# The middle 16-bit part of the row maxima taken from the PSUM bank in a one-core transformer block on Trainium2

## The chip, the core and the metric

The kernel runs on one core of one Trainium2 chip. A core has five instruction streams that run side by side and meet only at semaphores: TensorE (PE in the rows; its weight loads are shown as PEld), VectorE (DVE), ScalarE (ACT), GpSimd (POOL) and SyncE (SP, which here only issues DMAs). The metric is the device time of one execution in microseconds (us), as the median of the runs. A second figure, the span, is the time from the first to the last instruction of the one execution that was profiled.

## What is computed

The reference embeds a batch of 8 images of 1024 tokens with 29 features each to 128 channels, adds a position table, and runs one transformer block: attention with 8 heads of 16 channels over chunks with a causal mask, then a mixture-of-experts feed-forward layer.

```python
scores = jnp.einsum('bhqd,bhkd->bhqk', Q, K)
mask = (1.0 - causal) * -100000.0
attn = jax.nn.softmax((scores + mask) / math.sqrt(d), axis=-1)
out = jnp.einsum('bhqk,bhkd->bhqd', attn, V)
```

A softmax over 1024 keys needs the maximum of each row of scores. What the change touches is how that maximum is handed on.

## The kernel before

**Tiling.** An image `i` (8 of them) is worked through in two halves of 512 tokens. In attention, a unit `u` is a group of 4 heads of one half: 4 units for an image, 32 in all. The scores are made twice. The first time (`score`, L546) TensorE writes a 128-row tile into one of two banks `bank_s`, and VectorE takes the row maximum out of it (L784 with the mask for tiles on the diagonal, L780 without). The second time (`prob`, L576) the transposed scores, with the maxima already subtracted, go to one of two banks `bank_p`, and ScalarE takes the exponential (L1051); GpSimd zeroes what the mask hides (L1213), and `weigh` (L594) multiplies by the values.

**How the maxima travel.** The subtraction is part of the second matmul: queries and keys are stacked as 16-bit parts in `q_stack` and `k_stack`, and three extra rows of `q_stack` hold the maximum of each query as three bfloat16 parts that add up to the float32 value. The step is called `turn`: TensorE transposes the maxima of a unit into `bank_m` (L559), and VectorE splits them in four instructions (L798 to L804): the high part `mrow_h`, the remainder `mrow_r` in float32, its high part `mrow_m`, and what is left of it, `mrow_l`. Then SyncE issues three DMAs (L449), after which the first `prob` of the unit can run. `bank_m` is one bank, used in turn by embedding, projections, transposes, gates and shared layer; the semaphore `m_taken` says when VectorE or ScalarE has finished reading it, and the next step of TensorE that writes it waits for that.

**The rest of an image.** `emb`, `turn1`, `q`, `k`, `v` make queries, keys and values; `to`, `ant`, `oproj`, `z2t`, `gates`, `counts`, `shared` and the routing (`route`, parts 0 to 4, 19 small VectorE instructions, L872 to L923) stand behind attention; `in` (L480 to L482, then a tanh on ScalarE, L1089, and two VectorE products, `gate` L936 and `hid` L945) and `expert` (L682 to L684, L1107, L955) are the feed-forward layer, `combine` its weighted sum (L1113, L1243 to L1249).

**What sets the order.** Each engine's order is a string in the table `ORDER`, one letter for a step: s a score (or the merging of two maxima), p a prob, w a weigh or a take of its result, e load and embedding, a the projections, t the turn of maxima, b the steps behind attention, f feed-forward, h shared, c combine, d DMAs of stacked queries and keys, i steps done once at the start. The n-th letter of a kind stands for the n-th step of that stream, so a letter that moves among its neighbours moves a step past those of other streams. A wait in a step holds up all that stands behind it on its engine. The steps done once, on SyncE the loading of ten tensors of weights (`load_rest`, L423), on VectorE the rounding of the query and key weights (`front_weights`, L967 and L970), on ScalarE the filling of three rows of keys (`first_keys`, L1138), are placed by the letter i. At the very end TensorE runs filler matmuls (L492).

## Time and profile before

| | |
|---|---|
| median of 3 runs | 950.03 us (949.52 to 952.06) |
| the profiled execution | 951.46 us, span 949.7 us |
| mean granted TensorE clock | 0.984 |
| PE busy | 907.3 us (96%) |
| DVE busy | 786.0 us (83%) |
| ACT busy | 596.3 us (63%) |
| POOL busy | 374.8 us (39%) |
| scores on VectorE, L784 and L780 | 244.3 and 166.0 us |
| the four instructions of the split, L798 to L804 | 8.7, 8.9, 9.2 and 10.2 us |

Of the profiled execution, 1.8 us lie outside the span (951.46 against 949.7). TensorE's busy time counts a matmul as the time it takes alone, so that neighbours overlap in the rows; a wait then shows on the weight loads (PEld) before it shows on the matmuls. VectorE's order is a queue of its own, and a row with `[x <-y]` says that the engine sat idle x us until y was done.

### The profile page before, as it was taken

What the parts mean: (1) busy time and instruction counts of PE and PEld (TensorE: products, weight loads), DVE (VectorE), ACT (ScalarE), POOL (GpSimd) and SP (SyncE); (2) the same over time, 40 slices, a digit from 0 to 9 for tenths busy, and PEclk for the clock granted to TensorE, in tenths of its full rate; (3) what the DMA queues carried; (4) which work ended last, traced back from release to release, by engine and by line L of the source; (5) the groups of instructions that cost most, each with busy time, mean ns of one, the idle gap of its engine ahead of it and who ended that gap; (6) DMA issues with size and microseconds to landing.
All of it is one profiled execution on the core that took longest, in us unless ns stands there. A gap on an engine that the chain in (4) does not pass through costs nothing. (4 is left out here: it accounts for less than half of the span.)

```text
span 949.7 us, 17664 instructions
## 1 busy us (share of the span) xinstructions
PE 907.3 (96%) x5646; PEld 540.7 (57%) x5646; DVE 786.0 (83%) x2529; ACT 596.3 (63%) x1365; POOL 374.8 (39%) x526
## 2 busy tenths in 40 slices
PE   7788999899999999999999999999999999999996
PEld 7633356356575656457555756466564765555575
DVE  5799988798789888889889889898889998894543
ACT  1335675475857675775766675675767576776644
POOL 3713323323445335343354325344444234332424
PEclk9799999899999999999999999999999999999999
DMA  5231011200111001110102001110110101000000
GB/s 178 59 54 50 20 35 34 65 16 4 34 46 57 10 18 49 38 65 18 35 15 72 26 24 40 45 47 30 38 46 17 47 26 46 26 13 2 12 1 23
DMA packets 45980, 35.19 MB, mean 37 GB/s; under 512 B 10816, under 2 KB 44608, under 8 KB 45760
## 3 DMA queue, kind: packets, MB, share of 16 engines
q1 hardware_dynamic: 43680, 31.97, 10.5%
q10 hardware_dynamic: 2208, 2.10, 1.0%
q8 instruction: 45, 0.74, 0.4%
q14 instruction: 47, 0.39, 0.1%
HBM read 4.28 MB, written 4.19 MB: 9 GB/s over the span
## 5 line engine op out<-in xcount | busy, mean ns | idle before, releaser
L1051 ACT ACTIVATE pt<-bank_p 128x512 f32<-128x512 f32 (+3 forms) x768 | 349.9, 492 | 200.6 <-PE bank_p L576 178.5
L784 DVE CUSTOM_DVE_ANT_0 bank_s<-bank_s,causal 128x384 f32<-128x384 f32 (+3 forms) x512 | 244.3, 505 | 40.0 <-PE bank_s L546 37.2
L546 PE MATMUL bank_s<-k_stack,q_stack 96*128 96x512 bf16 (+3 forms) x768 | 236.0, 333 | 17.4 <-DVE mx L784 8.9
L576 PE MATMUL bank_p<-q_stack,k_stack 99*128 99x512 bf16 (+3 forms) x768 | 229.0, 332 | 6.9 <-ACT pt L1051 5.1
L780 DVE TENSOR_REDUCE mx_far<-bank_s 128x1 f32<-128x512 f32 x256 | 166.0, 682 | 20.6 <-PE bank_s L546 19.2
L1213 POOL TENSOR_SCALAR_AFFINE_SELECT pt<-pt 128x512 f32<-128x512 f32 x128 | 81.1, 636 | 206.7 <-ACT pt L1051 206.5
L594 PE MATMUL bank_w<-pt,v 128*32 128x512 f32 (+3 forms) x1536 | 155.2, 502 | 0.2 <-POOL pt L1213 0.2
L546 PEld LDWEIGHTS bank_s<-k_stack,q_stack 96*128 96x128 bf16 x768 | 72.1, 99 | 131.9 <-DVE mx L784 55.6
L576 PEld LDWEIGHTS bank_p<-q_stack,k_stack 99*128 99x128 bf16 x768 | 72.7, 99 | 117.6 <-ACT pt L1051 69.8
L682 PE MATMUL bank_f<-wex_h,hid_h 128*128 128x512 f32 x256 | 116.4, 455 | 0.8 <-DVE gate L936 0.7
L684 PE MATMUL bank_f<-wex_h,hid_l 128*128 128x512 f32 x256 | 101.4, 396 | 0.0
L683 PE MATMUL bank_f<-wex_l,hid_h 128*128 128x512 f32 x256 | 101.2, 395 | 0.0
L1113 ACT ACTIVATE sel<-sel,wsel 128x128 f32<-128x128 f32 x256 | 81.5, 399 | 15.5 <-DVE sel L955 15.5
L784 DVE DVE_READ_ACCUMULATOR2_ANT mx<- 128x1 f32 x512 | 72.0, 141 | 0.0
L594 PEld LDWEIGHTS bank_w<-pt,v 128*32 128x32 f32 x1536 | 36.4, 109 | 62.5 <-issue 47.4
L1243 POOL TENSOR_TENSOR sel<-sel 128x256 f32<-128x256 f32 x64 | 46.8, 731 | 59.4 <-ACT sel L1113 59.4
L1107 ACT ACTIVATE sel<-bank_f,gm 128x512 f32<-128x512 f32 x64 | 44.0, 687 | 41.5 <-PE bank_f L684 21.8
L480 PE MATMUL bank_f<-z2t_h,win_h 128*128 128x512 f32 x128 | 66.6, 520 | 3.3 <-DVE gate L936 2.0
L1234 POOL TENSOR_TENSOR hid_l<-hid,hid_h 128x512 fp32r<-128x512 f32 x32 | 41.0, 1284 | 71.9 <-ACT hid_h L1097 71.9
L955 DVE SCALAR_TENSOR_TENSOR sel<-bank_f,gm,sel 128x512 f32<-128x512 f32 x64 | 47.7, 746 | 26.1 <-PE bank_f L684 16.5
L682 PEld LDWEIGHTS bank_f<-wex_h,hid_h 128*128 128x128 f32 x256 | 48.4, 189 | 13.2 <-issue 1.4
L684 PEld LDWEIGHTS bank_f<-wex_h,hid_l 128*128 128x128 f32 x256 | 48.1, 188 | 11.2
(139 smaller groups left out, 1428.9 us busy)
## 6 DMA issues: line engine op xcount, KB each, us to landing
q_stack<-qk_h SPq DMA_DIRECT2D x96, 64.0 KB, 2.6
k_stack<-qk_h SPq DMA_DIRECT2D x84, 64.0 KB, 2.6
q_stack<-qk_m SPq DMA_DIRECT2D x64, 64.0 KB, 2.6
out<-h SPq DMA_DIRECT2D x16, 256.0 KB, 2.4
k_stack<-qk_m SPq DMA_DIRECT2D x56, 64.0 KB, 2.6
q_stack<-qk_l SPq DMA_DIRECT2D x32, 64.0 KB, 2.6
k_stack<-qk_l SPq DMA_DIRECT2D x28, 64.0 KB, 2.4
x_sb<-x_t SPq DMA_DIRECT2D x16, 64.0 KB, 2.4
```

Of the source, the lines that this page charges most:

```text
L480: nc.tensor.matmul(dst, wh, xh, start=True, stop=False)
L546: nc.tensor.matmul(s_bank[s % 2][:, 0:cols], q_stack[0:STACK, half, hd, t % HT * P:(t % HT + 1) * P], k_stack[0:STACK, hd, key_place(i, ha ...
L576: nc.tensor.matmul(p_bank[p % 2][:, q0:HALF], k_stack[:, hd, key_place(i, kt // HT), kt % HT * P:(kt % HT + 1) * P], q_stack[:, half, hd, ...
L594: mm = nc.tensor.matmul(w_bank[VW * j:VW * (j + 1), q0:HALF], v[:, i % 2, kt, first:first + VW], pt[:, k % PT_SLOTS, j, q0:HALF], start=(k ...
L682: nc.tensor.matmul(f_bank[g][:], hid_h[:, c, tok], wex_h[:, c, w], start=(c == 0), stop=False)
L683: nc.tensor.matmul(f_bank[g][:], hid_h[:, c, tok], wex_l[:, c, w], start=False, stop=False)
L684: mm = nc.tensor.matmul(f_bank[g][:], hid_l[:, c, tok], wex_h[:, c, w], start=False, stop=(c == HID // P - 1))
L780: nc.vector.tensor_reduce(mx_far[:, u, col:col + 1], s_bank[s % 2][:], AX.X, ALU.max).then_inc(s_taken, 1)
L784: nc.vector.tensor_tensor_reduce(src, src, causal[:, HALF - cols:HALF], 1.0, -3.0e38, ALU.add, ALU.max, mx[:, u, col:col + 1]).then_inc(s_ ...
L1051: nc.scalar.activation(pt[:, k % PT_SLOTS, j, q0:HALF], p_bank[p % 2][:, q0:HALF], ACT.Exp, scale=0.25).then_inc(exp_done, 1)
L1113: nc.scalar.mul(sel[:, t % 2, part], sel[:, t % 2, part], wsel[:, t, e:e + 1]).then_inc(weighted, 1)
L1213: nc.gpsimd.affine_select(out=d, in_=d, compare_op=ALU.is_ge, fill=0.0, base=0, pattern=[[0, G4], [1, P]], channel_multiplier=-1).then_inc ...
```

## The change

In the step `turn` on VectorE, the instruction that rounds `mrow_r` to `mrow_m` is taken out. In its place the difference of bank and `mrow_h` is made twice, first written as bfloat16 into `mrow_m`, then as float32 into `mrow_r`. No wait stands between these two. The signal that `bank_m` may be written again comes with the second.

```diff
                 nc.vector.tensor_copy(mrow_h[:, u, :], src).then_inc(mh_made, 1)
                 dve.wait_ge(mh_made, n + 1)
+                nc.vector.tensor_tensor(mrow_m[:, u, :], src, mrow_h[:, u, :], ALU.subtract).then_inc(mm_made, 1)
                 nc.vector.tensor_tensor(mrow_r[:], src, mrow_h[:, u, :], ALU.subtract).then_inc(m_taken, 1)
                 dve.wait_ge(m_taken, after(i, "turn", u))
-                nc.vector.tensor_copy(mrow_m[:, u, :], mrow_r[:]).then_inc(mm_made, 1)
                 dve.wait_ge(mm_made, n + 1)
                 nc.vector.tensor_tensor(mrow_l[:, u, :], mrow_r[:], mrow_m[:, u, :], ALU.subtract).then_inc(ml_made, 1)
```

All five strings of `ORDER` are written anew, each with the same letters as before. Against the string of before, 1104 of TensorE's 2224 letters stand in another place, by 0.8 of a place on average over all letters, the farthest by 27; on VectorE it is 424 of 1301, on ScalarE 420 of 1142, on GpSimd 154 of 318, on SyncE 70 of 123. The beginnings of two of them:

```diff
     "dve": (
-        "ieaaeaaaaaaaeasesssssssassssassssasessstsssasasssassssssssssassssastssssassssasssssassasssssassasstsssss"
+        "eaeiaaaaaaaaeasesssssssassssasssssasesstsssassassasssssssssassssssatssssasssssassssassassasssssassastssss"
...
     "act": (
-        "aaaddfaaiaddppppppppppapppppapppapppwppppppppppppawpppppppbpppappppppppppppppapppppppbppppppppfppwpappfpf"
+        "iaaaddfaaaddpppppppppppapppapppapppppppwppppppppwapppppppbppppappppppppppppppppppppbppppppppfppwpappff"
```

The first place is VectorE's `turn` of unit 0, the first of 32 like it. Before:

```order
71 L798 CAST mrow_h<-bank_m 16x128
72 L800 TENSOR_TENSOR mrow_r<-bank_m,mrow_h 16x128
73 L802 CAST mrow_m<-mrow_r 16x128
74 L804 TENSOR_TENSOR mrow_l<-mrow_r,mrow_m 16x128
```

And with the change:

```order
71 L798 CAST mrow_h<-bank_m 16x128
72 L800 TENSOR_TENSOR mrow_m<-bank_m,mrow_h 16x128
73 L801 TENSOR_TENSOR mrow_r<-bank_m,mrow_h 16x128
74 L804 TENSOR_TENSOR mrow_l<-mrow_r,mrow_m 16x128
```

The cast from SBUF is gone, and two readings of the bank stand side by side.

The second place is VectorE about 39 us into the execution, where the remainders of the second half's queries are split (L759, L761) between scores of image 0. Before:

```order
58 L784 ISA bank_s,mx<-bank_s,causal 128x512
59 L784 ISA mx 128x1
60 L759 CAST qk_m<-qk_r 128x512
61 L761 TENSOR_TENSOR qk_l<-qk_r,qk_m 128x512
62 L784 ISA bank_s,mx<-bank_s,causal 128x128
```

And with the change:

```order
58 L784 ISA bank_s,mx<-bank_s,causal 128x512
59 L784 ISA mx 128x1
60 L784 ISA bank_s,mx<-bank_s,causal 128x128
61 L784 ISA mx 128x1
62 L759 CAST qk_m<-qk_r 128x512
63 L761 TENSOR_TENSOR qk_l<-qk_r,qk_m 128x512
```

One small score has gone ahead of the two.

The third place is VectorE near the end, where part 4 of the routing of the last image's first half (L914 to L923) meets the last products of its `in` steps (L936, L945). Before:

```order
2031 L945 SCALAR_TENSOR_TENSOR hid<-gate,bank_f 128x512
2032 L936 SCALAR_TENSOR_TENSOR gate<-gate,bank_f 128x512
2033 L914 TENSOR_TENSOR topp<-eprob,top 128x16
2034 L915 TENSOR_REDUCE esum<-eprob 128x4
2035 L917 TENSOR_REDUCE tsum<-topp 128x4
2036 L919 SCALAR_TENSOR_TENSOR tden<-esum,tsum 128x4
2037 L921 RECIPROCAL trec<-tden 128x4
2038 L923 TENSOR_TENSOR wsel<-topp,trec 128x16
2039 L945 SCALAR_TENSOR_TENSOR hid<-gate,bank_f 128x512
2040 L936 SCALAR_TENSOR_TENSOR gate<-gate,bank_f 128x512
2041 L945 SCALAR_TENSOR_TENSOR hid<-gate,bank_f 128x512
2042 L816 RECIPROCAL rec<-bank_m 128x16
```

And with the change:

```order
2029 L936 SCALAR_TENSOR_TENSOR gate<-gate,bank_f 128x512
2030 L945 SCALAR_TENSOR_TENSOR hid<-gate,bank_f 128x512
2031 L936 SCALAR_TENSOR_TENSOR gate<-gate,bank_f 128x512
2032 L945 SCALAR_TENSOR_TENSOR hid<-gate,bank_f 128x512
2033 L914 TENSOR_TENSOR topp<-eprob,top 128x16
2034 L915 TENSOR_REDUCE esum<-eprob 128x4
2035 L917 TENSOR_REDUCE tsum<-topp 128x4
2036 L919 SCALAR_TENSOR_TENSOR tden<-esum,tsum 128x4
2037 L921 RECIPROCAL trec<-tden 128x4
2038 L923 TENSOR_TENSOR wsel<-topp,trec 128x16
2039 L816 RECIPROCAL rec<-bank_m 128x16
```

The six instructions of the routing now stand behind both `hid` products instead of ahead of them.

Three of the steps done once have moved too. On VectorE `front_weights` stands behind the second embedding (L720) instead of ahead of the first. On ScalarE `first_keys` is the first step instead of the one between the second half's `q` and `k`. On SyncE the two loads of image 1's tokens (L417, each waiting for an embedding on TensorE) stand ahead of the ten loads of weights (L423) instead of behind them.

## Rows read from the trace of the kernel before

**Rows 1.** Windows: us, then busy time (and count) of each engine, clock, DMA, GB/s.
```profile
100.00:850.00 750.00, 735.66 (x4670) 429.49 (x4669) 661.15 (x2163) 502.73 (x1165) 299.19 (x423) 1.00 0.11 34
```

**Rows 2.** Waits, TensorE's weight loads: us in total, times, longest.
```profile
PEld bank_p L576 <- ACT pt L1051: 69.8, 160, 1.8
PEld bank_s L546 <- DVE mx L784: 55.6, 131, 3.3
PEld bank_s L546 <- DVE mx_far L780: 32.5, 79, 1.7
```

**Rows 3.** Groups of VectorE instructions: busy us, mean ns, idle before.
```profile
L804 DVE TENSOR_TENSOR mrow_l<-mrow_r,mrow_m 16x128 bf16<-16x128 f32 x32 | 10.2, 318 | 1.1
L802 DVE CAST mrow_m<-mrow_r 16x128 bf16<-16x128 f32 x32 | 9.2, 287 | 1.1
```

**Rows 4.** The tile mrow_r: durations min/median/max in ns; then who waited for it.
```profile
L800 DVE TENSOR_TENSOR mrow_r<-bank_m,mrow_h x32: 278/279/280, 45.1 to 860.5; 16x128 f32<-16x128 f32 x32
L802 DVE CAST mrow_m<-mrow_r x32: 214/215/752, 45.4 to 860.8; 16x128 bf16<-16x128 f32 x32
L804 DVE TENSOR_TENSOR mrow_l<-mrow_r,mrow_m x32: 278/280/612, 45.6 to 861.5; 16x128 bf16<-16x128 f32 x32
...
  PEld bank_m L480: 0.7, 2
```

**Rows 5.** Timeline of VectorE, one turn: start us, us, instruction.
```profile
613.16 0.28 DVE L800 TENSOR_TENSOR mrow_r<-bank_m,mrow_h 16x128 f32<-16x128 f32 x1
613.47 0.21 DVE L802 CAST mrow_m<-mrow_r 16x128 bf16<-16x128 f32 x1
613.72 0.28 DVE L804 TENSOR_TENSOR mrow_l<-mrow_r,mrow_m 16x128 bf16<-16x128 f32 x1
```

**Rows 6.** Timeline of GpSimd and VectorE, another turn.
```profile
334.82 0.73 POOL L1243 TENSOR_TENSOR sel<-sel 128x256 f32<-128x256 f32 x1
334.88 0.75 DVE L802 CAST mrow_m<-mrow_r 16x128 bf16<-16x128 f32 x1
335.67 0.57 DVE L804 TENSOR_TENSOR mrow_l<-mrow_r,mrow_m 16x128 bf16<-16x128 f32 x1
```

**Rows 7.** Timeline of VectorE and TensorE in the first 12 us.
```profile
5.67 0.36 DVE L967 CAST wqk_h<-z 128x128 fp32r<-128x128 f32 x2 [1.64 <-DMA bk_sb<-bk]
6.07 0.49 DVE L970 TENSOR_TENSOR wqk_l<-z,wqk_h 128x128 fp32r<-128x128 f32 x2
7.65 2.05 PE L508 MATMUL bank_m<-tokw_sb,x_sb 128*128 128x128 f32 x8 [0.95 <-DVE h L720]
10.40 1.12 DVE L738 TENSOR_SCALAR z<-h,mv,rs 128x128 f32<-128x128 f32 x4 [1.58 <-POOL rs L1190]
11.43 0.69 DVE L720 TENSOR_TENSOR h<-bank_m,pos_sb 128x512 f32<-128x512 f32 x1
```

**Rows 8.** Timeline of GpSimd, VectorE and TensorE, 36 to 44 us.
```profile
36.68 4.51 POOL L1255 TENSOR_TENSOR wex_l<-hid,wex_h 128x2048 fp32r<-128x2048 f32 x1
39.25 2.22 DVE L759 CAST qk_m<-qk_r 128x512 bf16<-128x512 f32 x1
43.06 0.29 DVE L784 CUSTOM_DVE_ANT_0 bank_s<-bank_s,causal 128x128 f32<-128x128 f32 x1
43.46 0.23 PE L546 MATMUL bank_s<-k_stack,q_stack 96*128 96x128 bf16 x1 [3.14 <-DVE mx L784]
```

**Rows 9.** Timeline of SyncE's queue and ScalarE at the start.
```profile
9.86 0.43 SPq L423 DMA_DIRECT2D bgate_sb<-b_gate  x1
28.54 1.04 ACT L1118 CAST win_h<-gate 128x1024 fp32r<-128x1024 f32 x1 [9.41 <-issue]
35.36 3.60 ACT L1138 CAST k_stack<-minus 3x4096 bf16<-3x4096 f32 x1
47.08 0.69 ACT L1032 ACTIVATE qk_h<-bank_m,bk_sb 128x512 bf16<-128x512 f32 x1 [8.12 <-PE bank_m L482]
```

**Rows 10.** Timeline of VectorE and TensorE, 893 to 900 us.
```profile
893.42 0.17 DVE L914 TENSOR_TENSOR topp<-eprob,top 128x16 f32<-128x16 f32 x1
895.63 0.68 DVE L945 SCALAR_TENSOR_TENSOR hid<-gate,bank_f 128x512 f32<-128x512 f32 x1
896.36 0.50 PE L480 MATMUL bank_f<-z2t_h,win_h 128*128 128x512 f32 x1 [1.05 <-DVE hid L945]
899.26 0.26 DVE L816 RECIPROCAL rec<-bank_m 128x16 f32<-128x16 f32 x1 [1.15 <-PE bank_m L612]
```

More of the change, by code:

```diff
@@ new lines @@
+        "hpsspwwsppsapsspssfssfsswstpswpspsasssspwsspepsswtspsspppspspsppspsbsppspspsppspbssswssbwwssbpspwppsapsp"
+        "wsppbswpssbsfpfptpfppsswpfppsswsfspassfpfsspfspfssfssbwsbspfbssppfsspbspfspsbpssfppswptpswphpwpsbspwsbps"
+        "pappfppfpfbwwppfepspfspspfpspwppwppsfpspsfpspasppfppfspsapsfphssfpspstfswwwspspfbsspfpsbfpspsbfspsbsppsf"
+        "psawpwssppwwppsaspspwpspstpsppeppswwppsbspswspsaspsffbspfpsafspfsppwpfsspfpfwspspbfsbpspfbssppfbfpssbspf"
+        "psphwsspfbpsspwwsppstfspsfpfppssbppssfpsspfpsfspapswwspspfswsppftspwpspwpsfasspfpspsfpsapssfspsapssfbpsp"
@@ new lines @@
+        "fsshspsfstfssfppsespfswwwwsppsapssppwpspspassppsswspspssppswssppwpspbspsppwppsspbpwpspstppswpspbsppswsbp"
+        "pspspepspspwppaspspwsppwbpswsspbppfspsfssppfapwwpbfsfbpfssbpfppsfbspfbpspfsppshspfpsbfssftssfpssbsppsfsp"
+        "sapsffpssaswwwwspspfppfssptpfsspasppfsfpspsaspsfpspsfspspwwwwsppsfsbppsfpsspfspsphpsspwssfsppstfpssffpss"
+        "fssppesswwwpspsbspspsppbspspwppbpspwspsbpspspwwpeppssppasppwspsppwsptspwpspbswssassffspapfpsfsbpspffassp"
+        "pfspswpspfwpssbfsbfbspspfbspfbpspsfpphspspfbpswwpssptwspsfspbspspfppsapspfpspswpspswwsppfpfssppftssppfsp"
@@ new lines @@
+        "sappsswwwsppsfsppsfspspfpspaspsfsspfsppsassppfbfsshsspfstfspsfssefspswwppswwspsaspsspswspspasppswpspbpps"
+        "swsppbppspsptpwspspbwpspsbpssppasppwsppwppsasppwpbsppswssbspsfppswpfbspfbspfppbfppsfbsfpsfpsbfppsshpspfb"
+        "ssfssbfpsptfesswwppsswwspsfbppssfppsfasppsffpssppapspsfspwwwssptfsppawspspfspsfpsspapspsfppswwspsfwspspf"
+        "tppsfspsfpspshppssfsppsfppssfssfpspsfspesswwwwssppspssppsbppwpspbpwsppsapswspsppbswsbppssppstppwppsapwpp"
+        "spsppwpspbspswpssaspsfsfppsbspffsspefspspfassppfwwwssppbffspsbfbpspsfbpssfsspphspfsspptfpssbpsspffsapsww"
@@ new lines @@
+        "fssssbsbsstbshsssbbfabsbfffsbssfsfessfssfsafssfasashsssfstssafbsssbssfssbsbfssabssssssastssesssssssasffb"
+        "sbfssffbsfsabfsfbssabssfsbssbsbssfbhsssfsssstassfssfssfssbssfsfssbassbstfsfbsbfssasfssssassasfssssfshsst"
+        "ssfseafssassssassssssssssssassssbsssbsstsssssbssbesssbasssssbbssfsbfbsbafafsbfsfbsfssafbsbfssbhssssfssst"
+        "ssfssbsbsbsabsbfssasfsfsstsfsfsasfssfsssssasfssfsssssfssshssssftssfssssfessasssbssbssasssbbssesssbsassst"
+        "ssssssasfsfasffssbfssasfbsbbsffsbsbsfbsassfbbssbhssasssstfsssssbbssbssfssfasfssfsstssfsfbsabssssfssfsssf"
@@ new lines @@
+        "sasssfasssfshssstssfsseafssasssssssasssassbsssbssstssssbsbsassbassssssbsbbsbfsfbbffsbsfsfssffsbbssbhsfss"
+        "sssbstfbssebabssssbfssasfssassfsfsasfstssfssassfsfssssssafsfstssfssshssfssssfsssssfesassssssabssbsssasss"
+        "ssbssbtssbsasssssssasfsfssbfssfebssfbsfsbfabsfsssbabfssssafssshssstssbfsbssfbasssssssassftfssbssbssbbsba"
+        "ssfsfsfssfssssssfsassfsfsssssfstsshsssssfssssfssbssbsssssbbstsssssbssssssbssbfsbfbfbfssfssfssfssfsssfsss"
+        "fsstbbbbbhfbfbbbffffffffbbfbbbhbfffbfbfbffffbffbffhff"
@@ new lines @@
+        "apppppppwppppapppppppppppppwppppbpppppppppppappwppbppppfbpppfpbfpfpfpfpbppppfpppcfpbfcpppfapfbappwppppfp"
+        "pfpappfpppppfpfpcppppbfppppccfppppfcpfpcpcpwppppppppppbppppppwpppppapppppppppbwafpapffppffppppbpfppbfppc"
+        "fbpppppcpppbfppppfppppppappppfbpppfppwpppffpapfcppppfpppcppapppfbcfpppfccfpppcppappppwapppppppppppppppbp"
+        "ppppwapppppppppbppwpfpppbbpfpfppffppbfppppppfbcfppfpbppcppbcppfapfppppppafpwpfpapppfpppfppppfcppppfppppc"
+        "pfpppppfcpcfcppwppppppppppppapppbwppppppppppapppppppbppapfppfpfpfwppfppbfbppfppcfppbpcppppfpppcfacpppbpp"
@@ L199 @@
+        "cfapacccpaacppcpppppppapbabfafappbcbpcpfafpcacpccppcaapppcpbppppbaaffabapcbpcppfcafcpapacpcapcppapppcpbp"
+        "pbffabpabcapcppfafcpcpaccpcapappppppbppcbaaffaaccppbpbpfapcfpapcppccppppcpbppcbffppppbcbcpppfpfccabccbff"
         "cccccc"
```

70 lines of the change are left out of this document (19 added, 51 removed).

## Prediction

> **What bounds the kernel now.** I read the windows first, since the busy shares of the page mix the start, the long middle and the end. Between 100 and 850 us TensorE is busy for 735.66 of 750 us, VectorE for 661.15, ScalarE for 502.73 and GpSimd for 299.19 [rows 1]. The reader should see two things: TensorE is nearly full, with 14.3 us of idle time in 750, and VectorE is second at 88%. So this is a kernel of two engines that hold each other up: TensorE sets the end, and it gets late where VectorE or ScalarE is late.
>
> The waits say how often. TensorE's weight loads waited 131 times for a masked maximum and 79 times for an unmasked one, 55.6 + 32.5 = 88.1 us in all, and 160 times for an exponential, 69.8 us [rows 2]. There are 768 scores, so in 210 / 768 = 27% of them VectorE was the last to be ready. I use that share below as the price of VectorE's time: of a microsecond that VectorE saves somewhere in the middle, about a quarter reaches TensorE. The chain that ended last covers only the final stretch here and carries no term.
>
> **The edit, on VectorE.** It stands in 32 places. In a turn without disturbance the remainder starts at 613.16, the cast 0.31 us behind it, the last difference another 0.25 us later [rows 5]: 0.56 us from the first subtraction to the last. With the change the first subtraction writes the middle part, the second follows with no wait between, and the last waits for the second. Two subtractions of 128 elements with no wait between them stand in the trace as one row of 0.49 us (L970, [rows 7]); one alone takes 0.28 us (L800, [rows 4]), so the second starts about 0.21 us behind the first. The distance becomes 0.21 + 0.31 = 0.52 us, 0.04 us less: 32 x 0.04 = 1.3 us of VectorE's time. The instruction put in is the slower one (279 against 215 ns, [rows 4]); what pays for it is the step that no longer waits.
>
> A rule of the Trainium skill speaks against the change here: the page VectorE: DVE Perf Modes, section on the TRN2 errata, gives a fixed 120 cycles at 0.96 GHz for reading PSUM and 58 for SBUF, and its table of tiers lets a float32 copy in SBUF run twice as fast. By it, the exchange would cost (120 + 128 - 58 - 64) / 0.96 = 131 ns each time, 4.2 us of VectorE in all and a quarter of that, 1.1 us, on the path, an estimate; the trace has 64 ns, so the rows decide.
>
> **The edit, and GpSimd.** The cast is the only one of the four with a wide spread: 214 to 752 ns, where the subtraction that reads the bank keeps to 278 to 280 [rows 4]. One case shows why: GpSimd starts an instruction at 334.82 that lasts 0.73 us, and the cast that starts at 334.88 takes 0.75 us, until the other is done [rows 6]. In all, the cast took 9.2 us where 32 x 0.215 would be 6.9: 2.3 us held up. The last difference took 10.2 where 32 x 0.280 is 9.0: 1.2 us held up [rows 3, 4]. The first 2.3 us go away with the cast. But the last difference, which reads two tiles of SBUF, starts at about the same time after the turn as before and can meet GpSimd itself, as it did right behind the cast in that case (0.57 us, [rows 6]). Gain between 0 (all of it moves over) and 2.3 us; I take 1.2, half of it, since the difference has been held up half as much as the cast.
>
> The Trainium skill has a rule for this, in SBUF — State Buffer, section on who interferes with whom: a copy in a two-port mode locks GpSimd out or waits for it, while an instruction with two SBUF inputs collides only with GpSimd work that reads SBUF, and one with a single SBUF input never does. The trace agrees for the bank readers (278 to 280 ns). By it nearly all of GpSimd's work here would still catch the last difference.
>
> Together VectorE gets back 1.3 + 1.2 = 2.5 us; 27% of it on TensorE's path is **-0.7 us**, with bounds of 0 and -3.6 (all of 1.3 + 2.3 counted).
>
> **The edit, and the bank.** The bank is given back with the third instruction instead of the second, 0.21 us later. Two of 32 times something waited for this very signal [rows 4]: **+0.4 us**; the upper bound is 32 x 0.21 = 6.7 us, if the next user of the bank stood right behind each turn. I stay at the lower value, since the row counts those who do. The three DMAs of the maxima start 0.04 us earlier, which changes nothing.
>
> **The start.** Four instructions (0.36 + 0.49 us, [rows 7]) move from a place where VectorE was waiting anyway to one ahead of the normalisation. That one started at 10.40 with its input just ready. The second embedding is ready on TensorE at 9.70 and takes 0.69 us on VectorE; with 0.85 us behind it the normalisation starts at 11.25 and ends at 12.37. Before, the next step of TensorE waited until the embedding was added at 12.12: +0.25 us. Against it, the small score of 0.29 us that moves ahead of the cast at 39.25 is done while that cast could not run: GpSimd works from 36.68 to 41.19, the cast takes 2.22 us, and TensorE waits 3.14 us for the score behind it [rows 8]. That gives about -0.3 us. Sum: **0**, with bounds of +0.85 and -0.3. The loads of weights are issued 4.8 us later, as they now stand behind TensorE's second embedding; the last was issued at 9.86, and the first reader starts at 28.54 [rows 9], so this costs nothing until the delay is over 10 us. The 3.60 us of `first_keys` on ScalarE move out of a stretch in which ScalarE then idled 8.12 us [rows 9]: nothing either.
>
> **The end.** Part 4 of the routing starts at 893.42 and keeps `hid` until 895.63; TensorE waits 1.05 us for it at 896.36 [rows 10]. With the routing behind both products, `hid` can start right after the gate product, at about 893.5, and this wait is gone. What is late next is the routing itself: its 2.2 us now run after the last `hid`, to about 898.9, and the reciprocal behind it (L816) started at 899.26 before. So not all of 1.05 is kept; the stretch can move up by about 0.8 us before something else holds it: **-0.8 us**, bounds 0 and -1.05.
>
> **The shuffle.** The strings of the order keep their letters, and half of TensorE's stand elsewhere, by less than one place on average. No row prices that. What can be counted is who stands next to whom on TensorE: two probs in a row 178 times against 168, two scores in a row 173 against 175, two weighs in a row 47 against 55. The first gives ScalarE less time between its exponentials, the last gives it more. I take **0** and price both in the rivals.
>
> Sum: -0.7 + 0.4 + 0 - 0.8 + 0 = -1.1 us. The profiled execution had a span of 949.7 and took 951.46 us, 1.4 us over the median of 950.03; the same step from the median gives **948.9 us**.
>
> **Rivals.** (1) Faster. The weighs that stood next to each other are pulled apart at eight places and fill gaps in which TensorE waited for an exponential. One such wait costs 69.8 / 160 = 0.44 us [rows 2], eight of them 3.5 us: 948.9 - 3.5 = 945.4. For it: those waits, and VectorE's, add up to 158 us, so a few per cent less of them is enough. Against it: nothing in the counts for scores points that way. (2) Slower. The ten more pairs of probs each bring a wait of 0.44 us, 4.4 in all: 948.9 + 4.4 = 953.3. It comes out slower from the point where at least nine of the ten cost their wait. For it: ScalarE's waits are the largest single entry in the rows, and a prob needs the exponential of the one two before it. Against it: a pair is harmless if other work stands on both sides. (3) The edit does not do what it is for: the last difference takes over all the waiting for GpSimd. Then 1.3 us of VectorE's time remain, a quarter of it on the path, and the time is 948.9 + 0.3 = 949.2. By the skill's rule on two SBUF inputs this is what would happen. It falls in the same class as the forecast.
>
> **How the numbers follow.** A measurement of this kernel can tell about 0.3% from no change, 2.85 us: from 947.18 to 952.88. The forecast and rival 3 lie within it and get 0.41 together (0.29 and 0.12). Rival 1 gets 0.34, as the two terms with a known place point down. Rival 2 gets 0.25. The range goes below rival 1 by most of what the edit could give at its bound (945.4 - 2.4 = 943.0) and above rival 2 by some of the bank's bound (953.3 + 1.2 = 954.5).
>
> **What would show it.** The edit: the two subtractions from the bank at 279 ns each, starting 0.21 us apart; the last difference over 10.2 us in total if it takes over the waiting, near 9.0 if it doesn't. The bank: more than two waits on the signal of L801. The start: the first normalisation at about 11.25, and TensorE's wait of 3.14 us shorter by about 0.3. The end: no wait of TensorE before the last L480 of image 7's first half, and part 4 of the routing behind both L945. The shuffle: the sum of the weight loads' waits for exponentials above 74 us (rival 2) or below 66 (rival 1). The forecast is wrong if the windows between 100 and 850 us hold much more or less TensorE idle time than now, since I have put the shuffle at zero without a row for it.

## The result and the profile after

| | before | after |
|---|---|---|
| median of the runs | 950.09 us (949.52 to 952.06) | 943.4 us (941.0 to 945.0) |
| profiled execution | 951.46 us, span 949.7 | 941.0 us, span 939.0 |

The ratio is 0.9922, 95% interval 0.9908 to 0.9936: 7.4 us faster, where the forecast was 1.1 us and "no change". Three more measurements of the same kernel gave 942.3, 942.84 and 942.91 us (ratios 0.9918, 0.9918, 0.9914). The first measurement lies just inside the range of the prediction (943.0 to 954.5 us), the three repetitions just below it.

Two rows of the page after, the busy sum of TensorE and the granted clock in 40 slices:

```profile
PE 900.1 (96%) x5646; PEld 535.8 (57%) x5646; DVE 784.4 (84%) x2529; ACT 597.2 (64%) x1365; POOL 376.2 (40%) x526
...
PEclk9879999999999999999999999999999999999999
```

TensorE does the same 5646 matmuls in 900.1 us of busy time instead of 907.3. This one sum does not tell whether the clock was higher or whether less waiting is hidden in the rows: in the three repetitions it is 903.6, 904.5 and 901.2 us, in three more executions with the old table 907.9, 907.4 and 905.9. The window that answers to [rows 1], and the waits that answer to [rows 2] and to the last line of [rows 4]:

```profile
100.00:850.00 750.00, 740.34 (x4706) 434.82 (x4706) 665.02 (x2176) 506.55 (x1172) 302.37 (x427) 1.00 0.10 34
```
```profile
PEld bank_p L576 <- ACT pt L1051: 68.5, 161, 1.3
PEld bank_s L546 <- DVE mx L784: 57.0, 140, 3.3
PEld bank_s L546 <- DVE mx_far L780: 28.8, 71, 0.9
...
PEld bank_m L480 <- DVE mrow_r L801: 0.7, 3, 0.4
PEld bank_m L632 <- DVE mrow_r L801: 0.3, 1, 0.3
PEld bank_m L616 <- DVE mrow_r L801: 0.2, 1, 0.2
```

TensorE idles for 9.7 us of these 750 instead of 14.3; in the three repetitions for 10.4 to 10.9, in a second execution of the kernel before for 13.6. The waits for an exponential, on which both rivals of the prediction rested, have hardly moved (69.8 to 68.5). One turn and the groups of its instructions, VectorE:

```profile
602.98 0.28 DVE L800 TENSOR_TENSOR mrow_m<-bank_m,mrow_h 16x128 bf16<-16x128 f32 x1
603.18 0.27 DVE L801 TENSOR_TENSOR mrow_r<-bank_m,mrow_h 16x128 f32<-16x128 f32 x1
603.49 0.28 DVE L804 TENSOR_TENSOR mrow_l<-mrow_r,mrow_m 16x128 bf16<-16x128 f32 x1
```
```profile
L804 DVE TENSOR_TENSOR mrow_l<-mrow_r,mrow_m 16x128 bf16<-16x128 f32 x32 | 9.7, 303 | 1.1
L800 DVE TENSOR_TENSOR mrow_m<-bank_m,mrow_h 16x128 bf16<-16x128 f32 x32 | 8.9, 278 | 1.1
...
L801 DVE TENSOR_TENSOR mrow_r<-bank_m,mrow_h 16x128 f32<-16x128 f32 x32 | 8.6, 268 | 0.0
```

So the edit does in a turn what was forecast: 0.20 us between the two subtractions, 0.51 us to the last. The question is where 7 to 8 us come from.

### The profile page after: what moved, and what is told of

Its sections match the earlier page's. It is cut to its first block, busy times and chain, and to the rows that moved or that the text cites. A ratio compares the mean times of both kernels' runs of the same rounds, so it can differ in the third digit from the quotient of the medians.

```text
span 939.0 us, 17696 instructions
## 1 busy us (share of the span) xinstructions
PE 900.1 (96%) x5646; PEld 535.8 (57%) x5646; DVE 784.4 (84%) x2529; ACT 597.2 (64%) x1365; POOL 376.2 (40%) x526
## 4 chain that ended last, share of the span: by engine, by line
PE 84%; DVE 10%; ACT 2%; issue 2%; ACTq 1%; DMA 0%; SPq 0%; POOL 0%; POOLq 0%; DVEq 0%
PE bank_w L594 14%; PE bank_p L576 13%; PE bank_s L546 13%; PE bank_f L682 6%; PE bank_f L684 6%; PE bank_f L683 6%; PE bank_f L480 3%; PE bank_f L482 3%; PE bank_f L481 3%; PE bank_m L648 3%; DVE bank_s L784 3%; DVE mx_far L780 3%; PE bank_m L622 2%; PE bank_m L612 1%; PE bank_m L632 1%
## 5 line engine op out<-in xcount | busy, mean ns | idle before, releaser
L576 PEld LDWEIGHTS bank_p<-q_stack,k_stack 99*128 99x128 bf16 x768 | 71.6, 99 | 113.2 <-ACT pt L1051 68.5
L480 PE MATMUL bank_f<-z2t_h,win_h 128*128 128x512 f32 x128 | 66.9, 523 | 2.2 <-DVE gate L936 2.1
L684 PEld LDWEIGHTS bank_f<-wex_h,hid_l 128*128 128x128 f32 x256 | 48.1, 188 | 11.1
```

The costliest lines, as they stand in the source:

```text
L480: nc.tensor.matmul(dst, wh, xh, start=True, stop=False)
L576: nc.tensor.matmul(p_bank[p % 2][:, q0:HALF], k_stack[:, hd, key_place(i, kt // HT), kt % HT * P:(kt % HT + 1) * P], q_stack[:, half, hd, ...
L684: mm = nc.tensor.matmul(f_bank[g][:], hid_l[:, c, tok], wex_h[:, c, w], start=False, stop=(c == HID // P - 1))
```

## Experiments

"Worth" below is the ratio to the kernel before, measured on the same chip, less one, times 951 us; an interval of a ratio is about 1 us wide to either side.

**The split and the table of orders, apart.** The first kernel has the table of before and the new split, the second the reverse.

```diff
 # edit_alone (table of before)
-                nc.vector.tensor_tensor(mrow_r[:], src, mrow_h[:, u, :], ALU.subtract).then_inc(m_taken, 1)
-                dve.wait_ge(m_taken, after(i, "turn", u))
-                nc.vector.tensor_copy(mrow_m[:, u, :], mrow_r[:]).then_inc(mm_made, 1)
+                nc.vector.tensor_tensor(mrow_m[:, u, :], src, mrow_h[:, u, :], ALU.subtract).then_inc(mm_made, 1)
+                nc.vector.tensor_tensor(mrow_r[:], src, mrow_h[:, u, :], ALU.subtract).then_inc(m_taken, 1)
+                dve.wait_ge(m_taken, after(i, "turn", u))
```

> The split of the row maxima as in the changed kernel (middle part from the bank, no wait between the two subtractions), with the order strings of before. Theory A (the gain is in the new order): the edit is worth what the prediction gave it, -0.7 us on VectorE and +0.4 us on the bank, so about 949.8 us, ratio 0.999 to 1.000. Theory B (the edit itself carries it, since it ends waits of VectorE for GpSimd that pass to TensorE in full): 943 to 945 us, ratio 0.992 to 0.995.

> The order strings of the changed kernel, with the split of the row maxima as before (cast of the remainder in SBUF). Theory A: 943.5 to 944.5 us, ratio 0.993. Theory B: 949 to 950 us, ratio 0.999 to 1.000. If the two runs together do not make up the 0.992 of the changed kernel, the edit and the order need each other.

> The changed kernel once more, for its granted TensorE clock over time. In the profiled execution its clock stood at half its level for about 19 us in all (24 to 31, 41 to 47 and 56 to 67 us), against about 28 us in the kernel before. Theory C (the low clock stretches belong to the order, as the idle time before them does): the same stretches again, within 2 us each, and a time of 943 us. Theory D (they come by chance): other stretches in each execution, with times that follow them by a microsecond for each two of low clock.

> The kernel before once more, for the same question. Theory C: low clock again at 20 to 31, 44 to 50, 60 to 67, 88 to 94 and 181 to 189 us, span about 949. Theory D: the stretch at 181 to 189 us, in which the changed kernel gained 4 us on it, is missing or elsewhere, and the span is then 3 to 4 us shorter.

Measured: the split alone 951.8 us, ratio 1.0013 (1.0002 to 1.0023), +1.2 us. The table alone 944.78 us, 0.9944 (0.9930 to 0.9958), -5.3. Both together 942.3 us, 0.9918 (0.9903 to 0.9933), -7.8. The gain is in the table. One more execution of the kernel before took 952.76 us. Neither theory about the clock holds in full. Against C, half clock lay in part elsewhere in the second execution of the changed kernel and added up to 27.3 us instead of 17.1. Against D, in the kernel before the stretch near 180 us was there again, though for 3.4 us instead of 6.8, and the span was not shorter (951.0 us).

Because -5.3 and +1.2 do not add up to -7.8, the table alone and the changed kernel were measured once more side by side:

> The changed kernel once more, in more rounds. It is 942.3 to 943.4 us by the runs so far (-8). The new table alone gave -5.9 and the new split with the old table +1.1: added up, -4.8, 946.2 us. If the split and the table are worth their sum, this run comes nearer to 946; if they are worth more together than apart, it stays below 943.5.

> The new table of orders with the old split of the maxima, in more rounds. If the split has no worth of its own beside its +1.1 us with the old table, this is as fast as or faster than the changed kernel in the same batch, 942 to 943 us. If the split is worth something once the table fits it, this stays near 944.8 us, 2 us above the changed kernel.

> The changed kernel, beside the run with the new table alone. 942.8 us, as the 13 runs so far have it; what decides is the distance to the other run: about 0 if the split is worth nothing, 2 us below it if it is.

Measured: 942.84 us (0.9918) for the changed kernel; then, on one chip, 942.84 us (0.9914, 0.9900 to 0.9927) for the table alone and 942.91 us (0.9914, 0.9900 to 0.9927) for both. The two measurements of the table alone lie 2.9 us apart, more than their intervals allow, and I can't say why. What holds in each case: with the new table the split is worth between 0 and -2.5 us, and the table carries at least two thirds of the gain.

**The table cut by time.** At many places in the strings as many letters of each kind stand ahead in both tables, so a table can be put together from stretches of the one and of the other. The cuts, as positions in the strings of TensorE, VectorE, ScalarE, GpSimd and SyncE: 100 us is 167, 98, 67, 19, 15; 215 us is 468, 285, 218, 55, 30; 862 us is 2130, 1252, 1084, 306, 120. The split is that of before in all of them.

> The kernel before, with the table of orders of the changed kernel for the first stretch alone, to 100 us (73 of TensorE's letters, 19 of VectorE's, 15 of ScalarE's, 6 of GpSimd's and 9 of SyncE's stand elsewhere); from there on, and in the split of the maxima, it is the kernel before. With the whole new table the turn at 112 us came between 0.9 us earlier and level. Theory 'each stretch has its own gain': 949.1 us, between -1.8 and +1 against the kernel before, and the stretch at half clock between 180 and 190 us is there as before. Theory 'the start sets the phase of the clock': the stretch at half clock at 180 to 190 us is gone, and the time is 946 us.

> The kernel before, with the new order between 100 and 215 us alone (158 letters of TensorE, 43 of VectorE, 54 of ScalarE, 14 of GpSimd, 4 of SyncE). Theory 'each stretch has its own gain': the new order here leaves TensorE no stretch in which it is held up long enough to lose its clock; no half clock at 180 to 190 us, and 946.7 us (-3.4, as the turns at 165 and 205 us lay 3.5 us apart in what they gained). Theory 'the start sets the phase': half clock at 180 to 190 us as before, and the time within 1 us of before.

> The kernel before, with the new order between 215 and 862 us alone (726 letters of TensorE, 287 of VectorE, 249 of ScalarE, 109 of GpSimd, 45 of SyncE). No clock is at stake here: the granted clock is 1.00 throughout in both. Theory 'the shuffle closes gaps of TensorE': 946.1 us (-4, from the turns at 229 and 860 us, 4.1 us apart in what they gained with the new table). Theory 'the shuffle is worth nothing, as forecast': within 1 us of before. Half clock at 180 to 190 us as before in both.

> The kernel before, with the new order from 862 us on alone (14 letters of TensorE, 14 of VectorE, 16 of ScalarE): both halves' products of the last feed-forward part stand ahead of the last part of the routing, and the neighbours change. By the forecast -0.8 us (1.05 us of waiting gone, 0.25 given back behind it), 949.3 us. Rival: all of the 1.05 us and more is kept, -2 us or more, since the last transposed output came 2.4 us further ahead at 907 us with the new table, and 1.1 to 1.4 at 935.

| new order in | us | ratio (95%) | worth |
|---|---|---|---|
| 0 to 100 | 949.18 | 0.9978 (0.9969 to 0.9988) | -2.1 |
| 100 to 215 | 951.32 | 1.0007 (0.9994 to 1.0020) | +0.7 |
| 215 to 862 | 948.79 | 0.9973 (0.9960 to 0.9985) | -2.6 |
| 862 to the end | 950.04 | 0.9992 (0.9982 to 1.0002) | -0.8 |

The sum is -4.8 us, and the whole table has -5.3 and -8.2. Each entry is uncertain by about 1 us, so the sum by about 2. The forecasts that named the clock fell: order_100_215 was to reach 946.7 us without half clock near 180 us, and it took 951.32 with 3.4 us of it. Three further cuts follow up on this, and one kernel takes only the first letters:

```diff
 # start_only: first letters of VectorE, ScalarE, SyncE and TensorE
-    "dve": "ieaaeaa...    "act": "aaaddfaai...    "sp": "iee...
+    "dve": "eaeiaaa...    "act": "iaaaddfaa...    "sp": "eei...
 # and two neighbouring letters of TensorE: "...aaess..." to "...aases..."
```

> The kernel before, with the new order of the first steps alone: 2 letters of VectorE (the rounding of the query and key weights behind the second embedding instead of ahead of the first), 9 of ScalarE (the filling of three rows of keys first instead of ninth) and 3 of SyncE (the ten loads behind the second x instead of ahead of the first e). Forecast: 0 (between -0.3 and +0.85). Rival, from the traces: the rounding stood ahead of the first embedding's sum on VectorE (L720), which started at 6.1 us in all four kernels with the new start and at 6.7 to 6.9 in the six with the old one; then the first transposed maxima come 0.7 us earlier (43.6 against 44.2 to 44.4 us), and the time is 0.7 us lower, 950.2 us or a little less.

> The kernel before, with the new order up to 215 us and the old from there on. Theory 'the stretches add up': -1.8 (to 100 us) + 0.3 (100 to 215) = -1.5, 949.3 us, and half clock at 180 to 190 us in some form as in either part. Theory 'the clock takes both': the stretch at half clock at 180 to 190 us was there with either part alone and gone with the whole table, so it is gone here, and the time is 3 us lower than the sum, 946.3 us.

> The kernel before, with the new order between 485 and 620 us alone (164 letters of TensorE, 55 of VectorE, 47 of ScalarE, 25 of GpSimd, 11 of SyncE). In the trace with the new order from 215 to 862 us this stretch gained 1.3 to 1.5 us, of which two waits of TensorE for scores, 0.74 us at 504 and 0.99 us at 571 us, are 1.7. Theory 'a few waits in this stretch': 949.6 us (-1.4). Theory 'spread over the middle': -0.45 (135 of 647 us of the -2.2), 950.6 us.

> The kernel before, with the new order up to 262 us and the old from there on. If the part that was missing in the sum is a seam at 215 us, this gets the 2.2 us of the cut at 215, the 1.6 us that were lost behind it, and the 0.9 us that the new table gains between the turns at 229 and 270 us: -4.7, 946.3 us. If the parts of the table only work together, it stays near the 2.2 us of the cut at 215: 948.7 us.

Measured: the first letters alone 950.43 us, 0.9991 (0.9982 to 1.0001), -0.9. Up to 215 us 948.91, 0.9975 (0.9965 to 0.9985), -2.4. From 485 to 620 us alone 949.46, 0.9987 (0.9976 to 0.9998), -1.2. Up to 262 us 947.39, 0.9971 (0.9959 to 0.9982), -2.8, where -4.7 was expected if a seam at 215 us were all that is missing. In the traces the cut at 262 is 1.8 us ahead of the cut at 215 for the turns behind both; in the runs it is 0.4. So a seam exists in the traces, but in the runs it doesn't account for what is missing. For order_485_620 the expectations were -1.4 and -0.45; the interval (-2.3 to -0.2) holds both, so this run doesn't decide between them. The interval of the first letters reaches from -1.7 to +0.1.

Three places can be read. The first is the start. TensorE's first embedding and what VectorE does with it, in the second execution of the kernel before and in the changed kernel:

```profile
4.78 1.21 PE L508 MATMUL bank_m<-tokw_sb,x_sb 128*128 128x128 f32 x8
6.42 0.49 DVE L970 TENSOR_TENSOR wqk_l<-z,wqk_h 128x128 fp32r<-128x128 f32 x2
6.83 0.68 DVE L720 TENSOR_TENSOR h<-bank_m,pos_sb 128x512 f32<-128x512 f32 x1
7.67 1.13 PE L508 MATMUL bank_m<-tokw_sb,x_sb 128*128 128x128 f32 x8 [1.68 <-DVE h L720]
```
```profile
4.78 1.05 PE L508 MATMUL bank_m<-tokw_sb,x_sb 128*128 128x128 f32 x8
5.95 0.69 DVE L720 TENSOR_TENSOR h<-bank_m,pos_sb 128x512 f32<-128x512 f32 x1 [1.92 <-PE bank_m L508]
6.79 1.13 PE L508 MATMUL bank_m<-tokw_sb,x_sb 128*128 128x128 f32 x8 [0.95 <-DVE h L720]
```

In the first block the embedding is ready at 5.99 us, and VectorE comes to it at 6.83, because the rounding of the weights (L967, L970) stands ahead of it; without that it starts 0.1 us after TensorE ends. TensorE's second embedding waits for exactly this. It starts between 7.35 and 7.70 us in the eight executions with the old start. With the new start it starts between 6.79 and 7.36 in eight executions of twelve, and in the other four between 7.51 and 7.66, as late as with the old one. In those four the first embedding itself was slow, as here in the fourth measurement of the changed kernel:

```profile
4.78 1.92 PE L508 MATMUL bank_m<-tokw_sb,x_sb 128*128 128x128 f32 x8
6.81 0.69 DVE L720 TENSOR_TENSOR h<-bank_m,pos_sb 128x512 f32<-128x512 f32 x1 [2.78 <-PE bank_m L508]
```

The execution of [rows 7] was such a one too (1.91 us for these eight matmuls), so there the rounding cost nothing. The move saves up to 0.8 us, depending on how long the first embedding takes.

The second is the stretch from 485 to 620 us. With the old order there TensorE waits in order_from_862 at two scores:

```profile
504.92 0.60 PE L546 MATMUL bank_s<-k_stack,q_stack 96*128 96x512 bf16 x2 [0.74 <-DMA q_stack<-qk_l]
...
571.98 0.34 PE L546 MATMUL bank_s<-k_stack,q_stack 96*128 96x384 bf16 x1 [0.99 <-DVE mx L784]
```

With the new order in this stretch alone, neither is there: the longest wait for a score between 500 and 506 us is the one of 0.18 us below. But only one of the two belongs to the order. The wait of 0.99 us is there in all ten executions with the old order at this place and in none of the ten with the new. The wait for the DMA is there in four of those ten (0.34 to 0.89 us) and is missing in both executions of the kernel before. Between the turns at 455 and 651 us the stretch takes 195.1 us with the new order in it and 195.6 to 196.6 in nine executions with the old: about 0.8 us, where the runs had -1.2.

```profile
504.34 0.39 PE L546 MATMUL bank_s<-k_stack,q_stack 96*128 96x512 bf16 x1 [0.18 <-DVE mx_far L780]
```

The third is the end, told with the prediction's steps below.

**The clock.** The stretch from 165 to 200 us, windows as in [rows 1] (busy times, then the granted clock): the kernel before, the new order from 485 to 620 us only (so the old order here), the table alone (second run), and the changed kernel:

```profile
165.00:200.00 35.00, 31.43 (x189) 13.70 (x185) 29.18 (x96) 17.87 (x39) 12.19 (x18) 0.90 0.14 45
```
```profile
165.00:200.00 35.00, 31.38 (x203) 14.29 (x202) 31.86 (x106) 19.34 (x43) 14.48 (x21) 1.00 0.14 45
```
```profile
165.00:200.00 35.00, 31.67 (x193) 14.69 (x193) 31.83 (x105) 18.61 (x41) 11.41 (x16) 0.95 0.17 56
```
```profile
165.00:200.00 35.00, 32.42 (x206) 15.03 (x205) 32.57 (x114) 20.24 (x43) 10.98 (x15) 1.00 0.17 56
```

A clock of 0.90 means that TensorE ran at half its speed (1.2 instead of 2.4 GHz) for 6.8 of the 35 us, 0.95 for 3.4 us. The first two kernels are the same program up to 485 us: at the same place one execution had half clock for 6.8 us and the other not at all. From the turn at 175 us to the one at 205 us the old order takes 27.3 us without half clock (two executions), 28.5 and 28.7 with 3.4 us of it, and 29.5 to 30.1 with 6.8 us: 0.32 to 0.41 us of time for each us at half clock. Summed over 0 to 930 us:

| us at half clock | each execution | mean |
|---|---|---|
| old order to 215 us and split of either kind (before, before_again, edit_alone, order_215_862, order_from_862, before_bank_late, order_485_620) | 27.3, 37.5, 34.1, 34.1, 30.7, 30.7, 27.3 | 31.7 |
| whole new table (after and its three repetitions, order_alone twice, bank_late) | 17.1, 27.3, 27.3, 20.5, 27.3, 20.5, 23.9 | 23.4 |

The two means lie 8.3 us apart, but they are of 14 executions. Every run has a mean granted clock, and from it the time at half clock, 2 x (1 - clock) x span, here with the end behind 930 us: 31.1 us in 97 runs of the kernel before, 28.6 in ten of the table alone, 25.7 in 18 of the changed kernel, each mean good to about 1 us. So over all runs the difference is 2.5 us for the table and 5.4 for the changed kernel. Nor is 0.41 the price everywhere: among runs of the same kernel (236 in all) the time rises by 0.17 us for each us at half clock, and the clock accounts for about a third of their scatter. At 0.17 to 0.41, as an estimate, the clock is worth 0.4 to 1.0 us of the table's gain and 0.9 to 2.2 of the changed kernel's.

That the order decides the half clock near 180 us is not shown. It was granted in 5 of the 7 old executions and in 1 of the 7 new ones; but order_alone twice, order_to_215 and order_to_262 are one program until there, and three of the four had it (3.4 us each), while the changed kernel and bank_late, which differ from it by the split, had it in none of five. TensorE's busy time ahead of it does not tell the cases apart (31.43 and 31.38 of 35 us above), and what does stays open.

**Stretch by stretch.** The starts of the turns (L798) divide every trace at the same places in the work; the table names the 4th, 7th, 8th and 32nd of them by their time in the kernel before. In us, with the time at half clock in brackets:

| | old table | new table, split of before | changed kernel |
|---|---|---|---|
| start to the turn at 112 | 112.1 (20) to 115.7 (34) | 110.2 (17), 111.3 (27) | 110.1 (17) to 112.4 (27) |
| 112 to 175 (0) | 63.3 | 62.8 | 62.3 |
| 175 to 205, without half clock | 27.3 | 27.0 | 26.5 |
| 205 to 860 (0) | 653.5 to 654.6 | 651.2, 651.8 | 651.6 to 652.7 |
| 860 to the end | 89.5 to 89.6 | 88.5 | 88.5 to 88.7 |

With the same 27.3 us at half clock the first stretch takes 113.2 to 113.8 us in three executions with the old table and 111.3 to 112.4 in three with the new. So with the clock taken out the table gains about 1.5 + 0.5 + 0.3 + 2.6 + 1.1 = 6.0 us: the larger part of its gain is not clock. In the long stretch TensorE is busy for the same time and idles less (windows as in [rows 1], from the turn at 205 to the one at 860; the kernel before, then the table alone):

```profile
205.53:860.17 654.64, 645.76 (x4114) 387.25 (x4107) 576.63 (x1869) 444.68 (x1035) 266.54 (x378) 1.00 0.11 34
```
```profile
201.08:852.25 651.17, 645.72 (x4120) 387.66 (x4117) 577.04 (x1872) 444.36 (x1032) 266.27 (x377) 1.00 0.10 34
```

Idle time is 8.9 us in the first and 5.5 in the second, 8.0 and 8.2 in two more executions with the old table, 6.0 in the other one of the table alone. The new split, with the new table, saves 0.5 us in each of the two stretches between 112 and 205 us and costs about 0.8 us between 205 and 860: about nothing in all.

**The price of the bank.** In two kernels the bank of the transposed maxima is given back with the last difference:

```diff
 # before_bank_late (bank_late: the same in the changed kernel, from L801)
-                nc.vector.tensor_tensor(mrow_r[:], src, mrow_h[:, u, :], ALU.subtract).then_inc(m_taken, 1)
-                dve.wait_ge(m_taken, after(i, "turn", u))
+                nc.vector.tensor_tensor(mrow_r[:], src, mrow_h[:, u, :], ALU.subtract).then_inc(ml_made, 1)
+                dve.wait_ge(ml_made, n + 1)
...
-                nc.vector.tensor_tensor(mrow_l[:, u, :], mrow_r[:], mrow_m[:, u, :], ALU.subtract).then_inc(ml_made, 1)
+                nc.vector.tensor_tensor(mrow_l[:, u, :], mrow_r[:], mrow_m[:, u, :], ALU.subtract).then_inc(m_taken, 1)
 # and SyncE's wait ahead of the DMAs of the maxima names m_taken instead of ml_made
```

> The changed kernel, in which the bank of the transposed maxima is given back with the last difference (L804) instead of the second subtraction (L801), 0.52 us later in a turn, 32 times. By the forecast's price for this hold (0.4 us for 0.21 us, from the waits that name the signal), 1.0 us slower than the changed kernel, 943.9. If every turn has the next user of the bank right behind it, 32 x 0.52 = 16.6 us slower, 959 us. If nothing waits for it, within 0.5 us of the changed kernel.

> The kernel before, in which the bank is given back with the last difference (L804) instead of the remainder (L800), 0.56 us later in a turn, 32 times. By the forecast's price (0.4 us for 0.21 us) +1.1, 952.2 us. By the price that the same dose had with the new table (4.3 us for 0.52 us) +4.6, 955.7 us. If the old table leaves room behind a turn that the new one does not, below +1.

Measured: bank_late 947.14 us, 0.9957 (0.9945 to 0.9970), 3.7 us above the changed kernel beside it. before_bank_late 957.88 us, 1.0070 (1.0058 to 1.0083), +6.7. The expectation for bank_late had the dose wrong: in the rows of the turn above, L804 starts 0.31 us after L801, so the bank is held 0.31 us longer, not 0.52. Then the prices agree: 3.7 / (32 x 0.31) = 37% and 6.7 / (32 x 0.56) = 37%. Each time difference is uncertain by 1 to 2 us, so that the two come out equal is partly luck; but the stretch from the turn at 205 to the one at 860, at full clock and with 24 turns, has nearly the same prices: 3.1 of 7.4 us (42%) and 4.8 of 13.4 us (36%). Who waited for the signal in before_bank_late, against one line of 0.7 us, 2 times, before [rows 4]:

```profile
  PEld bank_m L480: 3.7, 6
  PEld bank_m L632: 1.7, 3
  PE bank_m L480: 1.4, 4
  PE bank_m L632: 0.9, 2
  PEld bank_m L529: 0.8, 1
  PEld bank_m L616: 0.6, 1
```

Eleven weight loads wait 6.8 us, where two waited 0.7. The waits that exist say nothing of those that stand just short of one.

**The dose turned round.** The first instruction copies the maxima out of the bank and gives it back; the split reads the copy:

```diff
+                nc.vector.tensor_copy(mrow_f[:], src).then_inc(m_taken, 1)
+                dve.wait_ge(m_taken, after(i, "turn", u))
-                nc.vector.tensor_copy(mrow_h[:, u, :], src).then_inc(mh_made, 1)
+                nc.vector.tensor_copy(mrow_h[:, u, :], mrow_f[:]).then_inc(mh_made, 1)
...
 # and both subtractions read mrow_f instead of src
```

> The changed kernel, in which a turn's first instruction copies the maxima in float32 out of the bank and gives it back; the four instructions of the split then read that copy. The bank is held for about 0.28 us instead of 0.8, 0.52 us less in 32 turns, and VectorE has one instruction and one wait more, 0.31 us in each turn. If the price of the hold is the same downwards as upwards (0.26 us for each us): -4.3 us; VectorE's 32 x 0.31 = 9.9 us at 27%: +2.7; together 941.3 us (-1.6). If the hold only costs once it is longer than the room behind a turn, the first term is nearly gone (the waits on L801's signal are 1.4 us in the changed kernel): -1.4 + 2.7, 944.2 us (+1.3).

Measured: 952.99 us, 1.0031 (1.0019 to 1.0043), some 11 us above the changed kernel: far worse than either expectation. Waits of TensorE's weight loads, and the groups of a turn:

```profile
PEld bank_s L546 <- DVE mx L784: 63.0, 139, 4.7
PEld bank_s L546 <- DVE mx_far L780: 32.7, 78, 1.0
```
```profile
L806 DVE TENSOR_TENSOR mrow_l<-mrow_r,mrow_m 16x128 bf16<-16x128 f32 x32 | 12.1, 377 | 1.1
L802 DVE TENSOR_TENSOR mrow_m<-mrow_f,mrow_h 16x128 bf16<-16x128 f32 x32 | 10.9, 339 | 1.1
L803 DVE TENSOR_TENSOR mrow_r<-mrow_f,mrow_h 16x128 f32<-16x128 f32 x32 | 10.8, 336 | 0.0
L800 DVE CAST mrow_h<-mrow_f 16x128 bf16<-16x128 f32 x32 | 10.0, 313 | 1.1
```

The same two subtractions take 339 and 336 ns out of SBUF and 278 and 268 ns out of the bank. The Trainium skill, page SBUF — State Buffer, section on who interferes with whom, has it that a VectorE instruction with two SBUF inputs collides with GpSimd's reads, that one with at most one SBUF input does not outside the two-port modes, and that a copy in a two-port mode shuts GpSimd out or waits for it. The rows agree with the first (339 and 336 ns), and the cast out of SBUF, 215 ns when undisturbed and 313 on average here, agrees with the last; that the cast runs in such a mode no row shows. An undisturbed turn is 0.25 us longer (1.35 against 1.10), 8 us in all, and held up by GpSimd are another 9.6 us (10.3, counted from 215, 280, 272 and 280 ns, against 0.7 in the changed kernel): 17.6 us of VectorE. TensorE's waits for maxima rise from 57.0 + 28.8 to 63.0 + 32.7, by 9.9 us.

That is 56% of VectorE's time in waits, but not in time of the kernel. From the turn at 205 to the one at 860, at full clock, the turns are 11.1 us longer on VectorE and TensorE's waits for maxima by 5 us, and the stretch takes 654.6 us instead of 652.3: 2.3 us, or 21%; with the at most 1.3 us that an earlier release could win there, 32%. The forecast's 27% lies between them. The larger part of the 11 us stands elsewhere: 6.8 us between the turns at 112 and 175 us (69.1 instead of 62.3), where this execution was at half clock for 10.2 us. Over its eleven runs this kernel has 37.4 us at half clock against 25.7 of the changed kernel, so that is no accident of one execution; whether VectorE's longer turns bring it on is not settled. What fell is the idea that an earlier release pays: the waits on L801's signal were 1.4 us in all, so there was no more to win.

## Why the prediction was wrong

**The step that failed is the shuffle**, "I take 0". The letters of the table, moved by less than one place on average, are worth 5.3 and 8.2 us in two measurements of the table alone. The traces give about 6.0 us with the clock taken out: 1.5 up to the turn at 112 us, 0.8 from there to 205, 2.6 from there to 860, all of it TensorE's idle time, and 1.1 at the end (0.8 of which the prediction had as a term of its own). The clock adds 0.4 to 1.0 us, as an estimate. What can be named within it is less: up to 0.8 us by the first letters, the one wait of 0.99 us near 572 us, and the end; which moved letters make up the rest of the start and of the middle stays open. I had looked for a price in pairs of neighbours; the prices that can be named were in other rows: the single waits of TensorE in the middle with their times, and the stretches at half clock, most of which lie ahead of the window of [rows 1], which begins at 100 us, while 6.8 us in 750 vanish in the rounding of its 1.00. The prediction's last sentence named the right sign of failure: TensorE's idle time between 100 and 850 us fell from 14.3 to 9.7.

**The rivals.** Rival 1 comes nearest in time (945.4), but that is luck, its reason is wrong: the waits for exponentials stayed at 68.5 us, inside its bounds of 66 and 74. Rival 2 is out by the same number. Rival 3, that the last difference takes over all the waiting for GpSimd, did not happen. With the table of before, where only the split differs, the cast goes and L804 rises from 10.2 to 10.4 us, by 0.2 of the cast's 2.3. The table alone moves the waiting about (cast 8.1 us, L804 11.2), and with both L804 has 9.7. The rows of edit_alone and of order_alone:

```profile
L804 DVE TENSOR_TENSOR mrow_l<-mrow_r,mrow_m 16x128 bf16<-16x128 f32 x32 | 10.4, 325 | 1.1
```
```profile
L804 DVE TENSOR_TENSOR mrow_l<-mrow_r,mrow_m 16x128 bf16<-16x128 f32 x32 | 11.2, 349 | 1.1
...
L802 DVE CAST mrow_m<-mrow_r 16x128 bf16<-16x128 f32 x32 | 8.1, 253 | 1.1
```

**The edit, on VectorE**: right in the turn, too small in what GpSimd gives back. The turn got 0.04 us shorter, and what GpSimd holds up fell from 2.3 + 1.2 us to 1.4 with the old table and to 0.7 in the changed kernel: with the 1.3 us of the turns 3.4 to 4.1 us instead of the 2.5 that I took. At the forecast's 27%, which the long stretch of early_copy bears out (21 to 32%), this is -0.9 to -1.1 us instead of -0.7.

**The edit, and the bank**: mis-sized, and by more. 32 x 0.21 us at 37% is +2.5 us instead of +0.4. I stayed "at the lower value, since the row counts those who do"; the row counts who waits now. Six waits of 1.4 us on L801's signal were there afterwards. Together that is about +1.5 us for the edit, where -0.3 was forecast and +1.2 (0.2 to 2.1) measured with the old table. With the new table it measured 0 and -2.5 us, and the traces have about 0; why it costs less there is not shown.

**The start**: forecast 0, measured -0.9 (-1.7 to +0.1). The step "move from a place where VectorE was waiting anyway" holds only where the first embedding is slow, as in [rows 7]; elsewhere they stood ahead of its sum. The first normalisation started between 9.55 and 10.41 us in twelve executions, not at 11.25: the second embedding, which took 2.05 us in [rows 7] and set that number, took 1.13 in the others. Of ScalarE's and SyncE's letters no cost shows, as forecast, though they were not measured by themselves: the last load is issued at 12.63 us, 2.8 us later and not 4.8, and its first reader starts at 26.20. The long wait behind GpSimd's 4.5 us went from 3.14 to 3.11 us, so the -0.3 there was not to be had.

**The end**: right. Forecast -0.8, measured -0.8 (-1.7 to +0.2) with the new order from 862 us alone, and in the traces the part behind the turn at 860 us is about 1 us shorter in every execution that has it. The rows that answer to [rows 10], of the changed kernel:

```profile
883.82 0.50 PE L480 MATMUL bank_f<-z2t_h,win_h 128*128 128x512 f32 x1
...
884.62 0.42 PE L480 MATMUL bank_f<-z2t_h,win_h 128*128 128x512 f32 x1
...
886.23 0.69 DVE L945 SCALAR_TENSOR_TENSOR hid<-gate,bank_f 128x512 f32<-128x512 f32 x1
886.84 0.45 DVE L914 TENSOR_TENSOR topp<-eprob,top 128x16 f32<-128x16 f32 x1
...
888.52 0.26 DVE L816 RECIPROCAL rec<-bank_m 128x16 f32<-128x16 f32 x1 [0.29 <-PE bank_m L612]
```

TensorE's matmuls do not wait ahead of either L480 (the weight loads do, by 0.18 and 0.19 us), part 4 of the routing stands behind the last `hid`, and the reciprocal follows.

## What to carry to other kernels

- When two engines are nearly full, a reshuffle is not zero because its displacements are small. List the single waits of the bounding engine with their times, and ask of each whether the moved letters stand next to it. Then look whether it returns in other executions: of two waits here the one of 0.99 us stood in ten of ten with the old order, the one of 0.74 us in four, and not in the kernel before.
- A count of present waits is a lower bound for the price of a longer hold: holding a shared bank longer cost 36 to 42% of the added time in both orders, though the waits on the signal were 0.7 us in 32 turns.
- Before calling a place on an engine free, read a second execution: the rounding ahead of the first embedding cost nothing in one and 0.7 us in the next.
- Before giving a gain to the clock, compare stretches of the same work with the same time at half clock, and take the mean clock of all runs rather than of the few that were traced: here the 14 traced executions alone, 8.3 us at the highest price of 0.41, would have given the clock 3.4 us, and all runs give it 0.9 to 2.2.

## What the runs showed of the hardware

The same program at the same place can run with or without a stretch at half clock (0.90 and 1.00 in 165 to 200 us). One us of it cost 0.32 to 0.41 us of time there, and 0.17 us on average over the runs of all kernels, where it makes about a third of the scatter between runs of one kernel. A subtraction of 16x128 elements out of the bank right behind another starts 0.20 us after it and takes 268 ns, and an undisturbed subtraction out of the bank takes 63 ns more than the cast out of SBUF (278 against 215), half of the 131 that the prediction worked out, as an estimate, from the section on the TRN2 errata of the page VectorE: DVE Perf Modes of the Trainium skill: the measurement decides.
